# Cross-attention in f32: every main-loop matmul as a 64x64 tile, passes of 512 queries, K, V and context resident

## The reference

```
Q = x @ W_Q;  K = ctx @ W_K;  V = ctx @ W_V          # 16 heads x 64
attn = softmax(Q K^T / 8)                            # per head, 1024 x 6404
out = (attn @ V) @ W_O + x
result = (out - mean(out)) / sqrt(var(out) + 1e-5)   # over the 128 columns
```

## Time and profile before

| | us |
|---|---|
| median of 3 runs | 1788.14 (1787.32 to 1790.1) |
| the profiled execution | 1787.58 |
| its span, first to last instruction | 1785.8 |
| PE matmul busy | 1764.0 |
| VectorE busy | 1096.8 |
| ScalarE busy | 866.9 |
| mean granted TensorE clock | 0.998 |

### The profile page before, as it was taken

The page is one execution under the profiler, slowest core; times in us unless marked ns, Lnnn a source line. Parts: engine busy times, 40 slices in busy tenths (PEclk is TensorE's granted clock), DMA queues, the critical chain, the costliest instruction groups (busy, mean ns, idle before and its releaser), DMA issues.

```text
span 1785.8 us, 30476 instructions
## 1 busy us (share of the span) xinstructions
PE 1764.0 (99%) x11046; PEld 600.1 (34%) x11046; DVE 1096.8 (61%) x1136; ACT 866.9 (49%) x959; POOL 21.3 (1%) x24
## 2 busy tenths in 40 slices
PE   9999999999999999999999999999999999999997
PEld 3333333333333333333333333333333333333334
DVE  4665555557556575556756666655675566665577
ACT  4544544554454445454445444545444544454552
POOL 0000000000000000000000000000000000000000
PEclk9999999999999999999999999999999999999999
DMA  2000000000000000000000000000000000000000
GB/s 77 18 12 18 13 20 18 12 18 20 13 18 18 12 21 19 12 18 14 18 19 17 12 18 16 19 18 12 19 20 13 18 18 12 16 19 12 18 1 13
DMA packets 21835, 31.11 MB, mean 17 GB/s; under 512 B 2160, under 2 KB 9328, under 8 KB 21744
## 3 DMA queue, kind: packets, MB, share of 16 engines
q1 hardware_dynamic: 21456, 29.32, 6.0%
q10 hardware_dynamic: 288, 0.59, 0.1%
HBM read 29.38 MB, written 0.52 MB: 17 GB/s over the span
## 4 chain that ended last, share of the span: by engine, by line
PE 98%; DVE 1%; issue 1%; DMA 0%; ACT 0%; POOLq 0%; POOL 0%; SPq 0%; ACTq 0%
PE s_ps L439 43%; PE o_ps L450 41%; PE v_ps L425 6%; PE kq_ps L415 6%; PE kq_ps L420 1%; PE v_ps L574 0%; PE kq_ps L574 0%; DVE inv_sum L853 0%; DMA ctx_ring<-in_ctxT 0%; PE o_ps L590 0%; DVE limits L816 0%; PE v_ps L590 0%; PE kq_ps L590 0%; PE o_ps L420 0%; POOLq L89 0%
## 5 line engine op out<-in xcount | busy, mean ns | idle before, releaser
L690 ACT ACTIVATE probs<-s_ps 128x1024 f32<-128x1024 f32 x816 | 790.8, 1021 | 867.0 <-PE s_ps L439 867.0
L803 DVE TENSOR_TENSOR sums<-sums,probs 128x1024 f32<-128x1024 f32 (+1 forms) x800 | 925.0, 1218 | 0.8 <-issue 0.8
L439 PE MATMUL s_ps<-q_sb,k_sb 64*64 64x512 f32 x6528 | 794.6, 602 | 7.8 <-DVE inv_sum L853 6.8
L450 PE MATMUL o_ps<-probs,v_ring 128*64 128x512 f32 x3264 | 746.2, 599 | 0.0
L790 DVE COPY v_ring<-v_ps 128x256 f32<-128x256 f32 (+1 forms) x209 | 87.5, 419 | 664.1 <-PE v_ps L425 664.1
L450 PEld LDWEIGHTS o_ps<-probs,v_ring 128*64 128x64 f32 x3264 | 215.7, 136 | 510.0 <-issue 508.9
L439 PEld LDWEIGHTS s_ps<-q_sb,k_sb 64*64 64x64 f32 x6528 | 212.2, 132 | 423.8 <-issue 395.5
L425 PEld LDWEIGHTS v_ps<-wv_sb,ctx_ring 128*128 128x128 f32 x816 | 116.4, 190 | 128.6 <-issue 126.5
L425 PE MATMUL v_ps<-wv_sb,ctx_ring 128*128 128x128 f32 x816 | 134.2, 286 | 0.0
L415 PE MATMUL kq_ps<-ctx_ring,wk_sb 128*128 128x512 f32 (+1 forms) x208 | 115.3, 636 | 0.4 <-DMA ctx_ring<-in_ctxT 0.4
L677 ACT ACTIVATE k_sb<-kq_ps 128x512 f32<-128x512 f32 (+1 forms) x104 | 61.3, 590 | 3.9 <-PE kq_ps L415 3.9
(11 more groups left out here) (45 smaller groups left out, 75.1 us busy)
## 6 DMA issues: line engine op xcount, KB each, us to landing
ctx_ring<-in_ctxT SPq DMA_DIRECT2D x96, 256.0 KB, 2.6
ctx_ring<-in_ctxT SPq DMA_DIRECT2D x8, 130.0 KB, 2.2
wk_sb<-in_wk SPq DMA_DIRECT2D x8, 64.0 KB, 2.0
xT_sb<-in_xT ACTq DMA_DIRECT2D x1, 512.0 KB, 5.0
wv_sb<-in_wv SPq DMA_DIRECT2D x8, 64.0 KB, 1.9
x_sb<-in_x SPq DMA_DIRECT2D x1, 512.0 KB, 5.4
wo_sb<-in_wo SPq DMA_DIRECT2D x1, 512.0 KB, 6.5
out<-y SPq DMA_DIRECT2D x4, 128.0 KB, 1.8
```

The lines of the kernel that those rows point to most:

```text
L439: last = nc.tensor.matmul(s_ps[keys, h, head * QH:(head + 1) * QH], k_sb[rows, cols + half * DH:cols + (half + 1) * DH], q_sb[rows, parity ...
L450: last = nc.tensor.matmul(o_ps[rows, q], v_ring[:, v_at[0], v_at[1], rows], p_view[:, p_slot, h, head * QH:(head + 1) * QH], start=start, ...
L690: nc.scalar.activation(p_view[:, p_slot, h, :], s_ps[:, h, :], ACT.Exp, scale=SCALE).then_inc(probs_ready, 1)
L803: nc.vector.tensor_tensor(out=sums[0:rows, parity, h, :], in0=sums[0:rows, parity, h, :], in1=p_view[0:rows, p_slot, h, :], op=ALU.add).th ...
```

## The change

The new kernel works in 16 passes (PASSES): a pass is one pair of heads and one half of the queries, 51 units of one chunk each. Every matmul up to the last denominators has 64 rows and 64 columns of the array. Where a contraction goes over 128 partitions (products, K, V, Q, denominators), each half of the rows is a matmul of its own and writes a PSUM bank of its own; the two banks are added when they are taken out. Scores had this shape before.

```diff
-            def pv(p_slot, v_at, start, stop):
-                for h in range(NQH):
-                    q = slice(h * QH, (h + 1) * QH)
-                    for head in range(2):
-                        rows = slice(head * DH, (head + 1) * DH)
-                        last = nc.tensor.matmul(o_ps[rows, q], v_ring[:, v_at[0], v_at[1], rows],
-                                                p_view[:, p_slot, h, head * QH:(head + 1) * QH], start=start, stop=stop)
-                last.then_inc(pv_done, 1)
+            def product(u):
+                t, c = u // CHUNKS, u % CHUNKS
+                if c == 0 and t > 0:
+                    pe.wait_ge(o_a_ready, t)
+                    pe.wait_ge(o_b_ready, t)
+                if c % BLOCK == 0 and t % 2 == 0:
+                    pe.wait_ge(work_ready, COUNT["v", t // 2, c // BLOCK])
+                pe.wait_ge(probs_ready, u + 1)
+                for rows in range(2):
+                    for head in range(2):
+                        last = nc.tensor.matmul(o_ps[part(head), rows, :], v_all[part(rows), c, part(head)],
+                                                probs[part(rows), u % RING, head * QH:(head + 1) * QH],
+                                                start=(c == 0), stop=(c == CHUNKS - 1))
+                last.then_inc(pv_done, 1)
```

```diff
+    def work_at(t, c):
+        pair, h = t // 2, t % 2
+        if c == 0 and t > 0:
+            return ("d", t - 1, 0)
+        if h == 0:
+            if t == 0 and c in (0, 1, 7):
+                return {0: ("k", 0, 1), 1: ("v", 0, 1), 7: ("q", 0, 1)}[c]
+            if c % 4 == 2 and (c + 6) // 4 < BLOCKS:
+                return ("k", pair, (c + 6) // 4)
+            if c % 4 == 0 and c >= 4 and (c + 4) // 4 < BLOCKS:
+                return ("v", pair, (c + 4) // 4)
+        elif pair + 1 < PAIRS and c in (34, 36, 38, 40, 42, 44):
+            n = (c - 34) // 2
+            return (("q", "q", "k", "v", "k", "v")[n], pair + 1, (0, 1, 0, 0, 1, 1)[n])
+        return None
...
+            def work(found):
+                kind, at, b = found
+                banks = banks_of(found)
+                if found not in FIRST:
+                    pe.wait_ge(work_ready, COUNT[found] - 1)
...
+                if kind == "d":
+                    pe.wait_ge(sums_done, CHUNKS * (at + 1))
+                if kind == "v":
+                    for m in range(cols_in(b) // P):
+                        for rows in range(2):
+                            for half in range(2):
+                                at_key = b * BK + m * P + half * DH
+                                last = nc.tensor.matmul(banks[rows][part(half), m * P:(m + 1) * P],
+                                                        ctx_all[part(rows), at_key:at_key + DH],
+                                                        wv_sb[part(rows), at * P:(at + 1) * P], start=True, stop=True)
+                    last.then_inc(work_done, 1)
+                    return
+                for rows in range(2):
+                    for head in range(2):
+                        if kind == "k":
+                            weights = wk_sb[part(rows), at * P + head * DH:at * P + (head + 1) * DH]
+                            moving = ctx_all[part(rows), b * BK:b * BK + cols_in(b)]
...
+                        last = nc.tensor.matmul(banks[rows][part(head), 0:n], weights, moving, start=True, stop=True)
+                last.then_inc(work_done, 1)
...
+            for u in range(UNITS):
+                if u + AHEAD < UNITS:
+                    scores(u + AHEAD)
+                found = work_at(u // CHUNKS, u % CHUNKS)
+                if found is not None:
+                    work(found)
+                product(u)
+            work(("d", PASSES - 1, 0))
```

```diff
+            def take_half(found):
...
+                act.wait_ge(work_done, COUNT[found])
+                nc.scalar.activation(target, banks_of(found)[0][:, 0:n], ACT.Copy).then_inc(work_half, 1)
+            def add_half(found):
+                target, n = target_of(found)
+                dve.wait_ge(work_half, COUNT[found])
+                nc.vector.tensor_tensor(out=target, in0=target, in1=banks_of(found)[1][:, 0:n],
+                                        op=ALU.add).then_inc(work_ready, 1)
+            def add_sums(u):
...
+                    dve.wait_ge(sums_done, u)
+                    nc.vector.tensor_tensor(out=sums[0:rows, t % 2, :], in0=sums[0:rows, t % 2, :],
+                                            in1=probs[0:rows, u % RING, :], op=ALU.add).then_inc(sums_done, 1)
```

More of the change, by code:

```diff
@@ L54, in cross_attention_kernel @@
     SUM_MOST, SUM_LEAST = 1e20, 1e-20
[L62 to L86, removed]
+    INV_PIECES = 2
+    INV_STEPS = (3, 5)
+    LIMIT_STEPS = (7, 9)
+    assert NQH == 2 and BLOCKS == 13 and TAIL_CHUNKS == 3 and QT == 8
+    def work_at(t, c):
[13 more added lines that the diff above has]
+        return None
+    FIRST = [("k", 0, 0), ("q", 0, 0), ("v", 0, 0)]
+    COUNT = {}
+    for found in FIRST + [work_at(t, c) for t in range(PASSES) for c in range(CHUNKS)] + [("d", PASSES - 1, 0)]:
+        if found is not None:
+            COUNT[found] = len(COUNT) + 1
     ctx = ExitStack()
@@ L205, in cross_attention_kernel @@
         g_attn_done = sem("g_attn_done")
[L208 to L241, removed]
-                    step(LOOP_CHUNKS * j + k, k, True)
-            for c in range(FIRST_STRAIGHT, CHUNKS, 2):
-                step(c, c, False)
@@ L578, in w_need @@
-            def w_need(pair, parity, first):
-                if first:
-                    return 48
-                return 24 * pair + (16 + 24 if parity else 48)
-            run_pairs(pe, pair_body)
+                nc.tensor.matmul(s_ps[0:DH, 0, 0:QH], ones[:, :], o_a[:, :], start=True, stop=True)
+            for found in FIRST:
+                work(found)
+            for u in range(AHEAD):
+                scores(u)
+            for u in range(UNITS):
+                if u + AHEAD < UNITS:
+                    scores(u + AHEAD)
+                found = work_at(u // CHUNKS, u % CHUNKS)
+                if found is not None:
+                    work(found)
+                product(u)
@@ new lines, in _ @@
+            last = PASSES - 1
+            dve.wait_ge(o_a_ready, PASSES)
+            dve.wait_ge(pv_done, UNITS)
+            nc.vector.tensor_tensor(out=o_a[:, :], in0=o_a[:, :], in1=o_ps[:, 1, :], op=ALU.add).then_inc(o_added, 1)
+            add_half(("d", last, 0))
+            for n in range(INV_PIECES):
+                invert_sums(last, n)
+            dve.wait_ge(o_added, PASSES)
+            dve.wait_ge(inv_ready, INV_PIECES * PASSES)
+            nc.vector.tensor_tensor(out=attn[:, PAIRS - 1, QH:NQ], in0=o_a[:, :], in1=inv_sum[:, :],
+                                    op=ALU.mult).then_inc(last_norm_done, 1)
```

543 lines of the change are left out of this document (202 added, 341 removed).

## The result

The changed kernel takes 1643.24 us (1642.64 to 1643.83, 4 runs), before 1787.98. The ratio is 0.9189, with a 95% interval of 0.9173 to 0.9205: 144.7 us less. The forecast was 1649 (1636 to 1695).

What follows compares the result with a forecast made beforehand. PE was taken to bound the kernel, by streamed work and gaps at shape changes. First matmul 5.7 + streamed work 1605.0 + startup 3 + DVE waits 7 + tail 26.8 = 1647.5 span; with 1.8 more, 1649 us, range 1636 to 1695.

Steps and rivals of the forecast that it cites:

- The gaps belong to the shape change: PE's main loop: 0.15 to 0.20 us lost at each change of tile shape, 138 us in all, would go.
- the 6.8 of waits at the pairs' ends: PE's 7 waits at pair ends, 6.8 us before, would go because scores and denominators cover the copies of o_ps.
- Rival B: Seams between PE groups: any change of group costs 0.16, +300 us, 1949; chance 0.05 in full, shared with Rival C.
- Its milder form: PE seams: only the first load exposed, about 0.05 each, +94 us, 1743; chance 0.06, shared with Rival C's milder form.
- The streamed work: PE's rounds of scores, products, K, Q, denominators and V sum to 1605.0 us, no different from before.
- The upper end of 1.716: Products: us per unit if the two row halves took turns; 0.858 was taken.
- V's short rounds: V projections: four loads and four matmuls per round in 0.11 us; 0.24 if nothing overlaps, +106 us.
- Rival A: V projections: rounds don't keep 0.11; at 0.19 +65 us, 1714; at 0.137, 1671; chance 0.10.
- Rival C: PE's instruction supply bounds at about 17,540 matmuls, 1911 us; chance 0.05 in full, shared with Rival B.
- PE's waits on DVE: Passes 2, 4, ... 14: projections wait for late DVE adds, about 1 us a pass, 7 us.
- The ledger: DVE's load less PE's time, unit by unit: +1.30, -0.63, +1.30, backlog 1.97, giving 7 us of PE waits.
- Startup and tail: Both ends of the kernel: 3 us of waits at the start, 26.8 us after the last denominators.

## Why the prediction was right

**The gaps belong to the shape change.** This step carried the gain, and it holds in every direction tried. 138 us were read from four run lengths and one pair of weight loads. The two profiled spans differ by 143.7 (1785.8 and 1642.1): these 138, the 6.8 of waits at the pairs' ends, which are gone as forecast, and about 1 the other way in the start, the tail and the waits on VectorE. With one old shape back the time rises by 250.7 (253 forecast from the same rows), with K and V back by 73.5 (75), with half the changes by 126.5 (127). Rival B asked for a cost of any seam; the profile after has none. Its milder form, an exposed first load, had the right size (0.05) and the wrong place: here it comes only behind a change of shape or a wait. Two changes were tried, 64*64 with 128*64 and 64*64 with 128*128, both in float32 at the upper clock level; other pairs of shapes were not.

**The streamed work is the same.** Products as four 64x64 keep the beat of 0.429 while they accumulate over 51 chunks in two banks (two rounds, 0.858). The upper end of 1.716 is out.

**V's short rounds.** 32 records in 0.88 us: 0.11 a round, the value taken. Rival A falls with it. So does the higher figure of the Trainium skill: by "TensorE: Matmul & The Clock Gate", section on 56 ns against 53.3 ns, a MATMUL decoded by ucode takes about 62 ns, and here 32 matmuls and 32 loads pass in 0.88 us, 27 ns a matmul. The same section has starts of small matmuls never less than about 25 ns apart. This trace doesn't agree: only the mean is 27 ns, while the four matmuls of a V round start 3 to 17 ns apart, mostly 7, and the next round 0.11 us after the first. So V's rate wasn't "just allowed" by that floor, as the prediction has it; the floor plays no part where four tiles run side by side, and V's round of 0.109 is about a quarter of the 0.429 of a round with four times the columns. Rival C, the supply of instructions, falls too.

**PE's waits on DVE: the one term mis-sized.** The ledger had 7 us, the trace 1.4. These are the loads that waited in the changed kernel:

```profile
PEld w_ps L392 <- DVE v_all L595: 7.4, 15, 0.7
PEld w_ps L375 <- DVE k_all L595: 7.1, 8, 1.3
```

A load's wait isn't lost time for PE until it outlasts the round before it: the 7.1 us of waits of V's loads include 1.3 at the start, which leaves 0.8 in each of seven passes, and there the V piece starts only 0.12 us late (233.79 for 232.81 + 0.86) and the K piece before it not at all. With the longer first rounds behind late loads (0.05 and 0.03) an even pass loses 0.20, seven of them 1.4. The ledger added the durations of VectorE's instructions. In the trace they overlap:

```profile
225.86 1.75 DVE L614 RECIPROCAL inv_sum<-inv_sum 128x256 f32<-128x256 f32 x1
227.52 1.16 DVE L607 TENSOR_TENSOR sums<-sums,probs 128x1024 f32<-128x1024 f32 x1
228.60 0.67 DVE L595 TENSOR_TENSOR v_all<-v_all,w_ps 128x512 f32<-128x512 f32 x1
229.19 1.22 DVE L607 TENSOR_TENSOR sums<-sums,probs 128x1024 f32<-128x1024 f32 x1
```

A reciprocal of 1.75 us is followed by the next instruction after 1.66, a sum after 1.08 to 1.13, an add of 0.67 after 0.59. With these DVE is 1.0 behind after unit 3 rather than 1.30, inside the 1.08 that an add has to spare, and about 1.2 behind after unit 5 rather than 1.97, 0.1 beyond it. The experiment with one long reciprocal shows that the mechanism itself was right: once DVE is later than this slack, PE pays for all of the rest.

**Startup and tail.** The start, by PE's timeline:

```profile
5.76 1.50 PE L392 MATMUL w_ps<-ctx_all,wk_sb 64*64 64x512 f32 x8 [0.56 <-DMA ctx_all<-in_ctxT]
7.08 1.04 PE L392 MATMUL o_ps<-xT_sb,wq_sb 64*64 64x512 f32 x8
7.94 1.06 PE L375 MATMUL s_ps<-wv_sb,ctx_all 64*64 64x128 f32 x32
9.56 1.96 PE L328 MATMUL s_ps<-q_sb,k_all 64*64 64x512 f32 x16 [0.56 <-DVE q_sb L595]
```

K to Q takes 1.32 instead of 0.86, which the forecast didn't have. The clock stood at its lower level: the four records of K's first round last 1.05 to 1.06 us, the later ones of this shape 0.59, and the trace has the granted clock at its upper level (2.4 GHz) only from 6.66 us on. In the kernel before it was there from 5.13, ahead of the first K at 5.72, with the same four matmuls at the start in both; in the repeat of the changed kernel from 4.45, and K to Q takes 0.88. So this term differs from execution to execution.

Scores come 0.75 late (9.56 for 7.94 + 0.87), and three later places lose 0.57, 0.67 and 0.74. The start loses 3.2 us in all; 3 were taken. That is in part luck: the four waits counted as 2.9 took 2.7, and the 0.46 of the clock made up for it. The end:

```profile
1614.57 1.09 PE L392 MATMUL w_ps<-sums,ones 64*64 64x512 f32 x8
...
1615.59 7.41 PE L415 MATMUL s_ps<-wo_sb,attn 128*128 128x128 f32 x64
...
1634.11 1.27 DVE L619 TENSOR_REDUCE limits<-inv_sum 128x1 f32<-128x512 f32 x2
```

Denominators of the last pass start 0.2 late, behind the last sums. They end near 1614.57 + 0.86 and a little for their exposed load, 1615.5, and the span ends at 1642.1: a tail of 26.6 against 26.8.

All in all: 5.8 + 1604.9 (0.858 a group and 0.873 a V block) + 3.2 + 1.4 + 0.2 + 26.6 = 1642.1, for a forecast of 5.7 + 1605.0 + 3 + 7 + 26.8 = 1647.5. The miss of 5.4 is the ledger of DVE; the other terms are each off by 0.3 or less.

## What to carry to other kernels

A page that says "PE 99% busy" may hide 8% of idle array: divide the start-to-start time of a run by its rounds, and look at what the seams with an excess have in common. Here each change of tile shape between matmuls costs 0.15 to 0.20 us and a change of operands, banks or lines costs none. So in this kernel, which PE bounds, it paid to bring everything in the inner loop to one shape, even at four times the instructions for K and V and with a second bank to add; VectorE and ScalarE had the time to spare. Where two shapes must stay, make the runs between them long. In a ledger of who comes too late, use the distances from start to start of the engine's instructions, not their durations.

## What the runs showed of the hardware

Matmuls can be dense: 32 matmuls and as many weight loads of 64x64 tiles passed in 0.88 us (14 ns an instruction), in straight code of 35,000 PE instructions, without a stall for instructions.

VectorE and GpSimd take turns when both work on two tensors in SBUF. In the changed kernel, two sums of VectorE, and the add of GpSimd that begins during the first:

```profile
216.46 1.22 DVE L607 TENSOR_TENSOR sums<-sums,probs 128x1024 f32<-128x1024 f32 x1
217.85 2.04 DVE L607 TENSOR_TENSOR sums<-sums,probs 128x1024 f32<-128x1024 f32 x1 [0.18 <-ACT probs L509]
```

```profile
216.69 2.13 POOL L303 TENSOR_TENSOR o_b<-o_a,o_b 128x512 f32<-128x512 f32 x1 [77.25 <-ACT o_a L540]
```

The first sum has GpSimd's add beside it for almost 1 us and still takes its 1.22. The add takes 2.13 and ends 1.14 after that sum; the next sum, begun meanwhile, takes 2.04 and ends 1.08 after the add. It is the same at all 30 instructions of GpSimd in the passes: each ends 1.12 to 1.14 after the sum in flight at its start, and the sum behind it 1.08 to 1.09 after GpSimd's end. So each seems to wait until the other's instruction is done, rather than both running slowly. In the kernel before, a product of the same size on GpSimd takes 1.27, at 13 of 16 places with VectorE idle, and once (at 1763.0) beside a reciprocal, which reads one tensor and isn't lengthened either. An add of VectorE with one input in PSUM, in GpSimd's time (at 233.06), takes its usual 0.67. The turns come twice a pass, and only VectorE's spare time pays for them here.
